# State modulation on transposed tiles by ScalarE and TensorE instead of GpSimd, a reordered set-up, finer waits in the first batch, and new order strings

## What is computed

```
ada = silu(c) @ Wada.T + bada                      # c: one row per batch
shift, scale, gate = split(ada, 3)
x_ssm = ln(x, norm1_g, norm1_b)
x_ssm = x_ssm * (1 + scale) + shift                # the modulation
skip = x_ssm
x_ssm = ln(x_ssm, norm2_g, norm2_b)
mz, mx = x_ssm @ Wz.T + bz, x_ssm @ Wx.T + bx
z1 = ssm(mz @ Wc1.T + bc1, ...)                    # per channel: h = dA*h + dBu; y = sum(C*h)
z2 = flip(ssm(flip(mz @ Wc2.T + bc2), ...))
out = (silu(mx) * z1 + silu(mx) * z2) @ Wf.T + bf + skip
return x + gate * out
```

## Time and profile before

| what | value |
|---|---|
| median of 3 runs | 4466.41 us (4466.0 to 4467.25) |
| profiled execution | 4488.16 us, span 4486.4 us |
| busy | PE 83%, DVE 91%, ACT 80%, POOL 87% of the span |
| granted clock of PE, mean | 0.92 |
| moved by DMA | 470.59 MB, mean 105 GB/s |

### The profile page before, as it was taken

One profiled execution on the slowest core, in us unless ns is written; L12 is line 12 of the kernel. 1 busy time (PEld: TensorE's weight loads), 2 busy tenths in 40 slices (PEclk: granted clock), 3 DMA queues, 4 the chain that ended last, 5 costly groups with the idle time before them and its releaser, 6 DMA issues.

```text
span 4486.4 us, 73259 instructions
## 1 busy us (share of the span) xinstructions
PE 3736.9 (83%) x26068; PEld 2466.1 (55%) x26068; DVE 4066.7 (91%) x5618; ACT 3601.2 (80%) x8614; POOL 3920.8 (87%) x1836
## 2 busy tenths in 40 slices
PE   4987888888888888888888888888888888888655
PEld 3664555555555555555555555555555555655333
...
GB/s 121 14 66 71 116 104 106 115 118 105 101 114 116 117 106 115 118 109 103 107 115 118 106 115 121 112 97 111 116 114 106 115 126 110 96 114 108 120 107 30
DMA packets 337533, 470.59 MB, mean 105 GB/s; under 512 B 55420, under 2 KB 165095, under 8 KB 337165
## 3 DMA queue, kind: packets, MB, share of 16 engines
...
## 4 chain that ended last, share of the span: by engine, by line
ACT 28%; DVE 21%; PE 19%; POOL 7%; issue 7%; DMA 1%; SPq 0%; POOLq 0%; DVEq 0%
ACT ps L697 10%; PE ps L171 10%; DVE ps L712 7%; DVE S_X L712 5%; POOL S_X L756 4%; ACT A_ring L472 4%; PE ps L376 3%; DVE S_X L727 3%; DVE A_sm L429 3%; PE ps L395 2%; POOL S_X L769 2%; PE ps L791 1%; ACT C_tmp L613 1%; ACT C_tmp L616 1%; ACT C_tmp L610 1%
## 5 line engine op out<-in xcount | busy, mean ns | idle before, releaser
L756 POOL TENSOR_TENSOR S_X<-S_slot,S_bc 128x1024 f32<-128x1024 f32 x1024 | 2398.8, 2365 | 52.6 <-DMA S_bc<-scr_bc 24.7
L697 ACT ACTIVATE ps<-S_slot,acol 128x256 f32<-128x256 f32 x4096 | 1735.3, 466 | 288.0 <-DVE S_X L727 258.2
L712 DVE TENSOR_TENSOR_SCAN ps<-ps,S_X 128x512 f32<-128x512 f32 x1088 | 1299.8, 1215 | 42.4 <-POOL S_X L756 21.9
L712 DVE TENSOR_TENSOR_SCAN S_X<-ps,S_X 128x512 f32<-128x512 f32 x960 | 1141.0, 1209 | 33.4 <-ACT ps L697 27.0
L769 POOL TENSOR_TENSOR S_X<-S_X,S_bc 128x1024 f32<-128x1024 f32 x480 | 1133.2, 2366 | 32.0 <-DVE S_X L712 32.0
L791 PE MATMUL ps<-S_X,sum 128*32 128x256 f32 x8192 | 652.1, 422 | 120.9 <-POOL S_X L769 97.0
L727 DVE TENSOR_TENSOR S_X<-ps,S_bc 128x512 f32<-128x512 f32 x1088 | 726.3, 678 | 12.1 <-DVE ps L712 0.5
L791 PEld LDWEIGHTS ps<-S_X,sum 128*32 128x32 f32 x8192 | 204.7, 115 | 413.9 <-issue 162.5
L429 DVE TENSOR_REDUCE A_sm<-ps 128x4 f32<-128x1024 f32 x256 | 311.8, 1218 | 49.9 <-PE ps L376 44.9
L395 PE MATMUL ps<-A_qP,A_kP 32*128 32x256 f32 x2048 | 300.6, 412 | 52.9 <-ACT A_ring L472 34.8
L171 PE MATMUL ps<-C_xT,wcz 128*128 128x256 f32 x1024 | 266.3, 405 | 80.9 <-DVE C_dd L573 80.7
...
## 6 DMA issues: line engine op xcount, KB each, us to landing
S_slot<-scr_dd SPq DMA_DIRECT2D x1024, 256.0 KB, 4.6
...
S_bc<-scr_bc SPq DMA_DIRECT2D x256, 256.0 KB, 6.2
...
```

The lines of the kernel that those rows point to most:

```text
L697: ins = a.activation(B["bank"][half_at(b, u, i)][:, n * T:(n + 1) * T], B["slot"][:, s, j, 0, :], ACT.Exp, scale=K.k["acol"][:, s, LINES * ...
L712: v.tensor_tensor_scan(line(x if u in ON_POOL else decay), line(decay), line(x), 0.0, ALU.mult, ALU.add).then_inc(S.scan.sem, 1)
L756: g.tensor_tensor(B["X"][:, u % RING], B["slot"][:, s, :, 1, :], rep(B["bc"][:, s, q, :], 1, LINES), ALU.mult).then_inc(S.b.sem, 1)
```

## The change

Four things are changed together.

1. The modulation is moved. PE turns the normed tile `C_xh`, ACT applies scale and shift to the turned tile (two Identity activations with per-partition columns from a new resident `mcol`), `xs` now holds the turned tile, PE turns it back into a PSUM bank, and DVE's and ACT's second norm read that bank. POOL's two operations and the load of `C_mod` are gone. The output product of the state layer adds the skip with four 128x128 products where it had two of 128x256.
2. In the set-up the biases' round trip is issued by ACT's queue instead of SP's, the mask arithmetic is put ahead of the wait for it, and scale and shift are computed as columns.
3. In the first batch `K.W.done` is replaced by marks for what a piece really reads. One wait is new: ACT's first piece with `C_tmp` (L610) of a batch waits for POOL's gate of the batch before.
4. All order strings are new.

```diff
-    pe, act, dve, pool = ["xT"], norm + [n + "b" for n in norm] + ["xT"], stat + [n + "b" for n in stat], ["m1", "m2"]
+    pe, act, dve, pool = ["xhT", "xs", "xT"], norm + ["xs"] + [n + "b" for n in norm] + ["xT"], stat + [n + "b" for n in stat], []
...
-    if b == 0:
-        p.wait_ge(K.W.dve, K.W.done)
+    p.wait_ge(S.act.sem, S.act.at(b, "xn1"))
+    turn_tiles(p, k["ident"], B["xh"], bank, S.pe)
+    yield
+    p.wait_ge(S.act.sem, S.act.at(b, "xs"))
+    turn_tiles(p, k["ident"], K.xs[:, b % 3], bank, S.pe)
+    yield
     p.wait_ge(S.act.sem, S.act.at(b, "xn1b"))
     turn_tiles(p, k["ident"], B["xh"], bank, S.pe)
     for s in range(2):
         q = str(s)
         yield
         p.wait_ge(S.act.sem, S.act.at(b, "u10" if s else "xT"))
+        if b == 0:
+            p.wait_ge(K.W.dve, K.W.mark["wd1" + q])
...
-    x, xs = K.A["x"][:, b % 2], K.xs[:, b % 3]
+    x, xs = K.A["x"][:, b % 2], lambda t: B["bank"][:, t * D:(t + 1) * D]
...
-    v.wait_ge(S.pool.sem, S.pool.at(b, "m2"))
+    v.wait_ge(S.pe.sem, S.pe.at(b, "xs"))
     for t in range(TT):
-        v.bn_stats(B["st"]["raw"][:, t, :], xs[:, t, :]).then_inc(S.dve.sem, 1)
+        v.bn_stats(B["st"]["raw"][:, t, :], xs(t)).then_inc(S.dve.sem, 1)
...
+    a.wait_ge(S.pe.sem, S.pe.at(b, "xhT"))
+    if b == 0:
+        a.wait_ge(K.W.dve, K.W.mark["mcol"])
+    if b >= 3:
+        a.wait_ge(K.land["out"].sem, K.land["out"].at(b - 3))
+    for c in range(KD):
+        ins = a.activation(K.xs[:, b % 3, c, :], bank[:, c * T:(c + 1) * T], ACT.Identity, scale=k["mcol"][:, b, c:c + 1], bias=k["mcol"][:, b, KD + c:KD + c + 1])
+    ins.then_inc(S.act.sem, 1)
+    yield
     a.wait_ge(S.dve.sem, S.dve.at(b, "mv1b"))
-    normalize(a, lambda t: K.xs[:, b % 3, t, :], B["xh"], st, k["eps"][:], S.act, b, post="b")
+    normalize(a, lambda t: bank[:, t * D:(t + 1) * D], B["xh"], st, k["eps"][:], S.act, b, post="b")
...
+        if b == 0:
+            a.wait_ge(K.W.dve, K.W.mark["bd" + q])
...
+            if b and s + h == 0:
+                a.wait_ge(S.pool.sem, S.pool.at(b - 1, "gate"))
...
-    yield
-    g.wait_ge(S.act.sem, S.act.at(b, "xn1"))
-    g.wait_ge(K.land["mod"].sem, K.land["mod"].at(b))
-    if b >= 3:
-        g.wait_ge(K.land["out"].sem, K.land["out"].at(b - 3))
-    g.tensor_tensor(xs, B["xh"][:], mo(0), ALU.mult).then_inc(S.pool.sem, 1)
-    yield
-    g.wait_ge(S.pool.sem, S.pool.at(b, "m1"))
-    g.tensor_tensor(xs, xs, mo(1), ALU.add).then_inc(S.pool.sem, 1)
...
+            if b + u + i == 0:
+                a.wait_ge(K.W.dve, K.W.mark["decay"])
...
+            if b + c == 0:
+                p.wait_ge(K.W.dve, K.W.done)
...
-        ins = matmuls(p, bk[:, t * D:(t + 1) * D], [(K.Sb["g"][:, b % 2, c, t * P:(t + 1) * P], k["wf"][:, c, :]) for c in range(KE)]
-                      + [(k["ones"][:, 0:P], k["bias"][:, K.at["wf"]]), (k["ident"][:], K.xs[:, b % 3, t, :])])
+        terms = [(K.Sb["g"][:, b % 2, c, t * P:(t + 1) * P], k["wf"][:, c, :]) for c in range(KE)] + [(k["ones"][:, 0:P], k["bias"][:, K.at["wf"]])]
+        for n, (lhs, rhs) in enumerate(terms):
+            p.matmul(bk[:, t * D:(t + 1) * D], lhs, rhs, start=n == 0, stop=False, skip_group_check=True)
+        for c in range(KD):
+            ins = p.matmul(bk[:, t * D + c * P:t * D + (c + 1) * P], K.xs[:, b % 3, c, t * P:(t + 1) * P], k["ident"][:],
+                           start=False, stop=True, skip_group_check=True)
...
-    if b:
-        q.wait_ge(S.pool.sem, S.pool.at(b - 1, "m2"))
-    else:
-        q.wait_ge(K.W.stored, 16)
-    q.dma_start(B["mod"][:], K.scr["mod"][b][0:2].partition_broadcast(P)).then_inc(K.land["mod"].sem, 16)
...
-    q.dma_start(B["gate"][:], scr["mod"][b][2].partition_broadcast(P)).then_inc(to, 16)
+    q.dma_start(B["gate"][:], scr["gate"][b].partition_broadcast(P)).then_inc(to, 16)
...
+            t.ready().wait_ge(vector, mark["allb"])
+            a.dma_start(scr["bias"].rearrange("(a n) -> a n", a=1), M["allb"][:]).then_inc(round3, 16)
+            a.wait_ge(round3, 16)
+            a.dma_start(M["rowsb"][:], scr["bias"].rearrange("(a n) -> a n", n=P)).then_inc(round1, 16)
+            a.wait_ge(vector, mark["bparts"])
+            a.dma_start(scr["bparts"].rearrange("i (a n) -> a i n", n=P), M["bparts"][:]).then_inc(round2, 16)
+            a.wait_ge(round2, 16)
+            a.dma_start(k["bias"][0:PARTS, :], scr["bparts"]).then_inc(stored, 16)
...
-            q.wait_ge(vector, mark["allb"])
-            q.dma_start(scr["bias"].rearrange("(a n) -> a n", a=1), M["allb"][:]).then_inc(round3, 16)
-            q.wait_ge(round3, 16)
-            q.dma_start(M["rowsb"][:], scr["bias"].rearrange("(a n) -> a n", n=P)).then_inc(round1, 16)
-            q.wait_ge(vector, mark["bparts"])
-            q.dma_start(scr["bparts"].rearrange("i (a n) -> a i n", n=P), M["bparts"][:]).then_inc(round2, 16)
-            q.wait_ge(round2, 16)
-            q.dma_start(k["bias"][0:PARTS, :], scr["bparts"]).then_inc(stored, 16)
...
+        mark["adaT%d" % n] = t.count(v.tensor_scalar(ada[:, n, :], bank("adaT%d" % n)[:, 0:NB], M["badac"][:, n:n + 1], 0.0 if n < KD else 1.0, ALU.add, ALU.add))
+    yield
+    evict("ada2", M["ada"], bank("ada2")[0:NB, 0:D])
+    for c in range(KD):
+        yield
+        t.count(t.ready().tensor_scalar(mcol[:, :, c], ada[:, KD + c, :], M["g1"][:, c:c + 1], None, ALU.mult))
+        yield
+        mark["mcol"] = t.count(t.ready().scalar_tensor_tensor(mcol[:, :, KD + c], ada[:, KD + c, :], M["b1"][:, c:c + 1], ada[:, c, :], ALU.mult, ALU.add))
...
-    for m in range(3):
+    for n in range(2 * KD):
         yield
         p.wait_ge(Z.dve, mark["wada7"])
-        product("ada%d" % m, NB, D, [(M["condT"][:, i, :], M["wadaT"][:, i, m * D:(m + 1) * D]) for i in range(KE)] + [(M["ones32"][:], M["bada"][:, m * D:(m + 1) * D])])
+        product("adaT%d" % n, P, NB, [(M["wadaT"][:, i, n * P:(n + 1) * P], M["condT"][:, i, :]) for i in range(KE)])
+    yield
+    product("ada2", NB, D, [(M["condT"][:, i, :], M["wadaT"][:, i, 2 * D:3 * D]) for i in range(KE)] + [(M["ones32"][:], M["bada"][:, 2 * D:3 * D])])
```

More of the change, by code:

```diff
@@ L645, in c_pool @@
     S, B = K.S["C"], K.C
[L646 to L656 removed]
+    wa = K.wa[:, b % 2]
     for s in range(2):
@@ L905, in s_sp @@
         q.wait_ge(K.land["dd_out%d" % s].sem, K.land["dd_out%d" % s].at(b))
+        if b + s == 0:
+            q.wait_ge(K.W.dve, K.W.done)
         if b:
@@ L944, in products_of_scans @@
 def products_of_scans():
-    names = ["wada%d" % n for n in range(8)] + ["ada%d" % m for m in range(3)]
+    names = ["wada%d" % n for n in range(8)] + ["adaT%d" % n for n in range(2 * KD)] + ["ada2"]
     names += ["wx%d" % i for i in range(KD)] + ["wf%d" % c for c in range(KE)]
@@ L1235, in _ @@
                 load("conditions", M["bada"][:], line("L2_cond_bada"))
-                for n, name in enumerate(("norm1_g", "norm1_b")):
-                    load("conditions", M["rows"][:, n, :], W["L2_cond_" + name].partition_broadcast(NB))
+                load("conditions", M["badac"][:], cols("L2_cond_bada"))
+                for n in "gb":
+                    load("conditions", M[n + "1"][:], cols("L2_cond_norm1_" + n))
                 load("scans", M["g2"][:], cols("L2_cond_norm2_g"))
@@ L1335, in w_dve @@
         mark["b" + n] = t.count(t.ready().tensor_tensor(out[:], out[:], M["b%sc" % n][:], ALU.add))
+    av = k["acol"][:].rearrange("p s g q -> p (s g q)")
+    yield
+    v.wait_ge(Z.act, 1)
+    mark["decay"] = t.count(t.ready().tensor_scalar(av, av, 300.0 / FAR, -1.0, ALU.max, ALU.mult))
     g2 = M["g2"]
@@ L1465, in w_sp @@
     yield
-    q.wait_ge(Z.dve, Z.mark["mod"])
-    q.dma_start(K.scr["mod"], K.wa[0:NB, 0, 0:3, :]).then_inc(Z.stored, 16)
+    q.wait_ge(Z.dve, Z.mark["ada2"])
+    q.dma_start(K.scr["gate"], Z.M["ada"]).then_inc(Z.stored, 16)
 WORK = {
@@ L1526 @@
+    "SP": "SSCACSSLSCSssTCACtss",
 }
@@ L1586, in allocate @@
     K.scr = {"pcol": dram("pcol", [NB, P, PCOLS]), "mask": dram("mask", [NB, 3, PARTS, T], BF16),
-             "bias": dram("bias", [nbias]), "bparts": dram("bparts", [PARTS, nbias], BF16), "mod": dram("mod", [NB, 3, D]), "x": dram("x", [NB, T, D]),
+             "bias": dram("bias", [nbias]), "bparts": dram("bparts", [PARTS, nbias], BF16), "gate": dram("gate", [NB, D]), "x": dram("x", [NB, T, D]),
              "dd": dram("dd", [NB, 2, KE, P, 2 * T]), "bc": dram("bc", [NB, 2, 2 * N, T])}
@@ L1617, in buffers @@
     C["st"] = stat_buffers(sb, "C")
-    C["mod"], C["dd"], C["tmp"] = sb("C_mod", [P, 2, D]), sb("C_dd", [P, KE, 2, T]), sb("C_tmp", [P, KE, T])
+    C["dd"], C["tmp"] = sb("C_dd", [P, KE, 2, T]), sb("C_tmp", [P, KE, T])
     C["dbc"] = sb("C_dbc", [ONE + 1, T])
```

119 lines of the change are left out of this document (56 added, 63 removed).

## The result

The changed kernel took 4430.12 us (median of 4, 4426.16 to 4431.48) against 4466.83 (4466.0 to 4471.68): ratio 0.9907, interval 0.9895 to 0.992. That is 36.7 us less; 4433 was forecast. The profiled execution of the changed kernel took 4430.37 us with a span of 4428.6.

What follows compares the result with a forecast made beforehand. The prediction took DVE to bound the periodic stretch, with POOL close behind. From a median of 4466.4 us it took 25 for the start, 8 for the periodic stretch and 0 for the end: 4433, range 4396 to 4462.

Steps and rivals of the forecast that it cites:

- The set-up: Before the second block: ACT issues the biases' round trip earlier than SP did; 10 us less, bounds 0 and 13.15.
- The first batch: Up to the first scan: fewer PE products, 11.2 us less; with the set-up, first scan at about 289.
- The periodic stretch: Some 27 repeating batches: shorter DVE waits, -0.3 us a batch, -8 in all, bounds -77 and +35.
- L1's sum leaving the cover: Periodic batches: L1's sum no longer covers DVE's wait for L0's residual sum; +0.6 us a batch.
- the output product's clock: Periodic batches: wx fills PE's gap before the output product, so slow-clock cases go; half of 0.9 gained, -0.45 a batch.
- The scans' wait: Periodic batches: DVE's scans waiting for decays, 0.9 us a batch, were to lose half through looser ACT order; -0.45.
- the removal alone is worth nothing: Periodic stretch: taking two operations and a wait off POOL gains nothing, as its ring of eight buffers hides them.
- the floor of 125.1: Periodic stretch: cost of a batch with all DVE waits gone, its work unchanged; at most 77 us to gain.
- (b): Rival: the periodic stretch gains more, half of 2.85 us of waits a batch, 38 us; 4403; chance 0.25.
- (c): Rival: the start's gain is hidden, DVE waits for PE's put-off products from 300 to 600 us; 4460; chance 0.10.
- (d): Rival: slower, exps ahead of FiLM wait for banks that DVE must free, delaying L0's sum; 4492; chance 0.10.
- The third: Sign of being wrong: DVE's idle time in the periodic stretch has moved to a place the prediction didn't name.

Runs made afterwards that it cites:

- the swap back: Changed kernel with the projection wx ahead of the turn of L0's normed tile again in PE's periodic order: 4473.1 us, 128.0 a batch.
- experiment 3: Changed kernel with the old periodic order: 4523.8 us; kernel before, old operations, with the new periodic order: 4464.1 us.
- experiment 6: Changed kernel, same instructions, with all engines following the periodic order from batch 1 of the scans: 4389.6 us; from batch 2: 4401.5 us.

## Why the forecast came out

**The set-up (-10).** Right at the place, by another way: the second block starts 8.5 us earlier, and the bias wait fell from 13.15 to 5.33 (under 3 was expected; the trip took 9.7 us here, from ACT's issue at 43.28 to 53.01, and not 5.6). The prediction let FiLM and the parts of the masks "follow unchanged" and gave the trip's move nearly all of the gain. Alone it gives 1.6, since a product came in the wait's place, as the lower bound of this term had allowed. What made the sum right is the masks' split ahead of L3's FiLM products, for which there was no term.

**The first batch (-11 on PE, first scan at 289).** Wrong. The first scan starts at 305.97. Seven profiles with the new first order, or its same beginning, have it at 300.3 to 316.3, six with the old at 300.4 to 310.3. Two things failed.

The count: it ran up to the first sum over states, which starts at 327.84 in the kernel before, 17.5 us behind the first scan, and its 11 us were taken as a gain ahead of that scan. Up to L1's first output product PE has only 16 f32 products of 256 columns fewer, against 24 narrow ones more, about 2 us at the prediction's own costs. And behind it nothing was gained: from this product to the first scan are 65.3 to 67.9 us in the new order and 65.4 to 68.8 in the old.

The clock, which had no term. From the second block's start to L1's first output product the changed kernel takes 7.5 us longer, at a lower mean granted clock (the seventh number: 0.81, and 0.86 in the first profile of before). Changed kernel, this stretch and 20 us of it:

```profile
80.73:240.65 159.92, 146.95 (x773) 110.73 (x773) 70.34 (x173) 48.84 (x109) 4.11 (x3) 0.81 0.04 9
90.00:110.00 20.00, 19.89 (x66) 14.52 (x66) 4.58 (x16) 2.57 (x6) 0.00 (x0) 0.50 0.01 1
```

Before:

```profile
89.22:241.68 152.46, 140.79 (x757) 103.09 (x757) 67.11 (x164) 51.60 (x118) 3.80 (x3) 0.86 0.05 12
90.00:110.00 20.00, 16.37 (x75) 10.71 (x76) 10.25 (x28) 3.61 (x10) 0.00 (x0) 0.84 0.06 15
```

So the 8.5 us of the set-up are lost again here, most of them from 90 to 110 us. Over all profiles the stretch takes 150.6 to 163.1 us at 0.77 to 0.89 in the new first order, and 144.0 to 153.7 at 0.84 to 0.93 in the old. Length times clock gives 126 to 133 us at full clock and 129 to 134: an estimate, by which the new order has some 3 us less to do on average. Why the clock falls earlier in the new order is not shown. The end of batch 0 is 16 us earlier all the same (446.9, and 442.9 to 457.1 in the seven profiles, against 459.5 to 473.6 in the six). One part of it is forecast and holds in every profile: from the first scan to the second direction's are 28 us instead of 36. Which edit gives the other 8 was not separated.

**Batches 1 to 4 (0).** The step that failed: nothing was costed, because the orders were compared at the first scan and in the periodic stretch only. They cost 26 us.

**The periodic stretch (-8).** The places were right and their terms mis-sized. L1's sum leaving the cover was costed at +0.6 and the output product's clock at -0.45 a batch; the swap back, which undoes only the second, measured 1.97. It had been costed as 0.9 us in half of the batches; with the swap the wait rises by 1.8 a batch. The scans' wait, costed at half (-0.45), went from 0.9 to 0.4. That "the removal alone is worth nothing" was wrong in the new order: giving POOL the work back cost 0.75. And the floor of 125.1, from listed waits alone, was not one: over 22 batches the listed waits fell only from 2.8 to 2.1 a batch, and the batch by 1.8. Of the remaining 1.1, 0.3 lie in gaps too short to be listed and 0.8 in the closer overlap of DVE's instructions, which experiment 3 finds with the new order in either case.

**The second statistics.** In the changed kernel they read PSUM (1623.31 to 3890 us):

```profile
L571 DVE BATCH_NORM_STATS2 C_raw<-ps 128x6 f32<-128x256 f32 x36 | 13.7, 423 | 0.1
```

423 ns against 405: 0.04 us a batch, within the bounds from the rows. The Trainium skill (VectorE: DVE Perf Modes, section on the TRN2 errata) would have had 65 ns more for each; the measurement of 18 decides.

**The rivals.** (b), half of the waits, described the periodic stretch better than the forecast, though not its 4403. (c) named a loss behind the start, but neither its place nor its cause: it lies from 577 to 993 us and not from 300 to 600, and experiment 6 shows that the products put off do not make it. (d), exps ahead of FiLM, did not come: L0's sum waits 0.8.

Of the prediction's own signs of being wrong, the first two did not come: L0's sum waits under 2, and 400 to 600 us give nothing back. The third did in small part: DVE's waits for L1's softmax sums (`A_sm`) rose from 5.4 to 11.5 us, in a place that it had not named. The total fell in the range since errors covered one another; the range had not been built on such a pair.
